# Parked-table writes moved from ScalarE's queue to SyncE's, and one row scaling moved from ScalarE to VectorE, in a vision-tower kernel

## What is computed

```python
lu, ru, ld, rd = _shifts(x)                          # four diagonal shifts by half a patch
concat = jnp.concatenate((x, lu, ru, ld, rd), axis=1)
normed = (concat - mean) * rsqrt(var + EPS)          # one mean and variance per image
normed = normed * gamma[None] + beta[None]
y = conv_general_dilated(normed, W, (8, 8), 'VALID') + b    # 169 patches, 128 features
h = concatenate([cls_tok, y])                        # 170 tokens
h = h + attention(layernorm(h))                      # S += LR * v k^T per token; out = S q
h = h + ffn(layernorm(h))
```

## Time and profile before

| | |
|---|---|
| Median of 3 runs | 220.32 us (219.75 to 221.87) |
| The profiled execution's own time | 220.32 us |
| Its span, first to last instruction | 218.1 us |
| Outside the span | 2.2 us |
| TensorE busy | 197.3 us (90%) |
| GpSimd / VectorE / ScalarE busy | 153.8 / 152.9 / 127.6 us |
| Mean granted clock of TensorE | 0.982 of full speed |

### The profile page before, as it was taken

One profiled execution on the slowest core, in us unless ns is written; L12 is line 12 of the kernel. 1 busy time (PEld: TensorE's weight loads), 2 busy tenths in 40 slices (PEclk: granted clock), 3 DMA queues, 4 the chain that ended last, 5 costly groups with the idle time before them and its releaser, 6 DMA issues.

```text
span 218.1 us, 5079 instructions
## 1 busy us (share of the span) xinstructions
PE 197.3 (90%) x1566; PEld 168.0 (77%) x1566; DVE 152.9 (70%) x762; ACT 127.6 (59%) x312; POOL 153.8 (70%) x129
## 2 busy tenths in 40 slices
PE   0699997998999999999999999999999999999820
PEld 0489895886888889888888888889988888888610
DVE  4548875480576685769686687796696686699892
ACT  4322545699433545556755575745755565677982
POOL 1029946697993799969899939957999632445571
PEclk9999999999999999999999999999999999999975
DMA  5999992931305004234135252022022022010356
GB/s 142 388 424 420 416 423 86 221 165 28 150 0 165 5 3 162 54 87 148 31 70 187 47 169 50 3 50 51 0 48 51 2 51 48 19 32 3 77 120 150
DMA packets 17074, 25.90 MB, mean 119 GB/s; under 512 B 1576, under 2 KB 13551, under 8 KB 16920
## 3 DMA queue, kind: packets, MB, share of 16 engines
q1 hardware_dynamic: 16300, 25.06, 36.0%
q10 hardware_dynamic: 748, 0.51, 0.8%
HBM read 19.65 MB, written 5.92 MB: 117 GB/s over the span
## 4 chain that ended last, share of the span: by engine, by line
PE 69%; DVE 9%; DMA 9%; SPq 3%; issue 3%; POOL 3%; ACT 1%; POOLq 0%; ACTq 0%; DVEq 0%
PE conv L560 34%; PE vr_ps L608 12%; DMA images<-x_rows 9%; PE first_ps L618 9%; PE outs L635 8%; PE turn L593 4%; DVE dve L1232 2%; DVE state L983 2%; DVE state L975 2%; PE conv L568 1%; ACT scaled L773 1%; DVE images L1004 1%; POOL rstd L1325 1%; SPq L477 1%; DVE ln_stats L1012 1%
## 5 line engine op out<-in xcount | busy, mean ns | idle before, releaser
L560 PE MATMUL conv<-scaled,wt 128*128 128x256 f32 (+3 forms) x432 | 111.5, 374 | 7.4 <-DMA wt<-weight 7.1
L460 POOL TENSOR_TENSOR scaled<-rows,gam 128x832 f32<-128x832 f32 (+1 forms) x54 | 83.9, 1574 | 18.1 <-DMA rows<-x_windows 17.9
L560 PEld LDWEIGHTS conv<-scaled,wt 128*128 128x128 f32 x432 | 71.7, 193 | 15.4 <-DMA wt<-weight 7.1
L803 ACT ACTIVATE values<-vr_ps,rstd 128x256 f32<-128x256 f32 x76 | 36.0, 474 | 60.5 <-PE vr_ps L608 50.3
L1309 POOL TENSOR_TENSOR rstd<-var,powers 128x8 f32<-128x8 f32 (+2 forms) x20 | 30.4, 1519 | 26.6 <-DVE var L995 26.4
L975 DVE TENSOR_TENSOR state<-first_ps,state 128x128 f32<-128x128 f32 x76 | 22.1, 291 | 29.9 <-PE first_ps L618 25.0
L811 ACT ACTIVATE images<-images,ln_shift,ln_gain 128x128 f32<-128x128 f32 x80 | 37.3, 489 | 1.5 <-DVE ln_shift L1052 0.7
L1299 POOL TENSOR_TENSOR g_low<-g_t,g_high 128x512 fp32r<-128x512 f32 x21 | 26.7, 1273 | 7.0 <-ACT g_high L790 7.0
L608 PE MATMUL vr_ps<-w_high,g_low 128*128 128x256 f32 x77 | 30.7, 398 | 1.0 <-ACT values L803 0.9
L964 DVE BATCH_NORM_STATS2 ln_stats<-images 128x6 f32<-128x128 f32 x85 | 23.6, 285 | 5.1 <-ACT images L797 5.0
L983 DVE TENSOR_TENSOR state<-second_ps,state 128x128 f32<-128x128 f32 x76 | 21.5, 283 | 2.1
(11 more groups left out here) (197 smaller groups left out, 276.5 us busy)
## 6 DMA issues: line engine op xcount, KB each, us to landing
rows<-x_windows SPq DMA_DIRECT2D x12, 864.0 KB, 5.1
out<-images SPq DMA_DIRECT2D x40, 128.0 KB, 2.4
images<-x_rows SPq DMA_DIRECT2D x4, 832.0 KB, 14.7
images<-x_rows SPq DMA_DIRECT2D x1, 1040.0 KB, 14.1
images<-x_rows SPq DMA_DIRECT2D x1, 624.0 KB, 21.1
rows<-x_windows SPq DMA_DIRECT2D x1, 448.0 KB, 6.2
gam<-gamma SPq DMA_DIRECT2D x1, 422.5 KB, 7.0
bet<-beta SPq DMA_DIRECT2D x1, 422.5 KB, 7.5
```

What stands on the lines that cost most here:

```text
L460: return eng.tensor_tensor(scaled[:, s, at + skip:at + N], window[:, skip:N], gains.unsqueeze(2).to_broadcast([P, N - skip, B]), ALU.mult)
L560: last = pe.matmul(conv_ps[g % 2][:, at:at + n * B], held, scaled[:, s, a % RING:a % RING + n], start=first, stop=(g < EARLY and s >= TOP ...
L803: act.activation(values[:, t % VALUE_SLOTS].rearrange("p a e -> p (a e)"), vr_bank(t)[:, 0:2 * E], ACT.Identity, scale=rho_of(t)).then_inc ...
```

## The change

Two edits that don't touch each other. ScalarE no longer issues the two parked writes; SyncE does, behind the loads of rows 3 and 4 and ahead of its wait for them. And (4, 4) is no longer scaled by ScalarE token by token in the steps -3, -2 and -1, but by VectorE with one instruction in step -2, with a semaphore of its own (scaled_by_vector). (4, 3) stays on ScalarE.

```diff
-BY_SCALAR = ((2, 4), (3, 4), (4, 3), (4, 4))
+BY_SCALAR = ((2, 4), (3, 4), (4, 3))
+BY_VECTOR = ((4, 4),)
-ROW_4_TOKENS = {-7: (3, 0, 5), -6: (3, 5, 4), -4: (3, 9, 4), -3: (4, 0, 4), -2: (4, 4, 4), -1: (4, 8, 5)}
+ROW_4_TOKENS = {-7: (0, 5), -6: (5, 4), -4: (9, 4)}
...
             if (last, s) in BY_SCALAR:
                 eng.wait_ge(scaled_by_scalar, BY_SCALAR.index((last, s)) + 1)
+            elif (last, s) in BY_VECTOR:
+                eng.wait_ge(scaled_by_vector, 1)
...
             load_row(3)
             load_row(4)
+            for blk in range(2):
+                count = P if blk == 0 else PATCHES - P
+                sp.wait_ge(table_low_ready, blk + 1)
+                sp.dma_start(parked[blk * P:blk * P + count], term_parts[0:count, blk].bitcast(F32)).then_inc(terms_parked, 16)
             sp.wait_ge(terms_zero, 1)
             sp.wait_ge(terms_parked, 32)
...
             act.copy(w_high[:], w_vr[:]).then_inc(w_high_ready, 1)
-            for blk in range(2):
-                count = P if blk == 0 else PATCHES - P
-                act.wait_ge(table_low_ready, blk + 1)
-                act.dma_start(parked[blk * P:blk * P + count], term_parts[0:count, blk].bitcast(F32)).then_inc(terms_parked, 16)
             group_out(1)
...
+                if t == -2:
+                    for r, s in BY_VECTOR:
+                        dve.wait_ge(row_in[r % ROW_SLOTS], 16 * (r // ROW_SLOTS + 1))
+                        dve.wait_ge(gamma_in, 16)
+                        dve.wait_ge(conv_step, SHIFTS * last_group_of_row(r - 2) + s + 1)
+                        scale_shift(dve, r, s).then_inc(scaled_by_vector, 1)
```

More of the change, by code:

```diff
@@ L153, in pool_scales @@
 def pool_scales(r, s):
-    return SHIFTS * (r - 1) + s + 1 - len([at for at in BY_SCALAR if at <= (r, s)])
+    return SHIFTS * (r - 1) + s + 1 - len([at for at in BY_SCALAR + BY_VECTOR if at <= (r, s)])
 FIRST_SCALES = (-7, -5, -4, -3, -2)
@@ L171 @@
 LATE_SCALES = [(r, s, scale_step(r, s)) for r in range(EARLY_ROWS, N) for s in range(SHIFTS)
-               if (r, s) not in BY_SCALAR + ((N - 1, BOTTOM + 1),)]
+               if (r, s) not in BY_SCALAR + BY_VECTOR + ((N - 1, BOTTOM + 1),)]
 def tower(nc, x_rows, x_windows, first_offsets, first_gamma, gamma, beta, weight, top_weight, last_row, smalls, bias, owners, cls_tok,
@@ L315, in tower @@
         scaled_by_scalar = sem("scaled_by_scalar")
+        scaled_by_vector = sem("scaled_by_vector")
         corner_scaled = sem("corner_scaled")
@@ L470, in load_row @@
                     sp.wait_ge(scaled_by_scalar, len([at for at in BY_SCALAR if at[0] <= r - 3]))
+                    if r - 3 >= EARLY_ROWS:
+                        sp.wait_ge(scaled_by_vector, 1)
                     if r - 3 >= CORNER // N:
@@ L840, in step @@
                 if t in ROW_4_TOKENS:
-                    s, first, count = ROW_4_TOKENS[t]
+                    first, count = ROW_4_TOKENS[t]
                     for j in range(first, first + count):
-                        last = scale_part(EARLY_ROWS, s, j)
+                        last = scale_part(EARLY_ROWS, SHIFTS - 2, j)
                     if first + count == N:
```

## The result

The changed kernel takes 218.88 us (median of 20 runs), the kernel before 220.19 us on the same chip; the ratio is 0.9933, 95% interval 0.9912 to 0.9954. So it gains 0.67% by the ratio and 1.31 us by the medians, where 2.06 were forecast (the ratio is not the quotient of the two medians). One of the 20 runs took 403.51 us and is not in the ratio; without it the median is 218.84. The profiled execution has a span of 216.8 us, 1.3 less than before.

The account below looks back on a forecast made before the run. TensorE was taken as the bound from 52 to 190 us, carrying any earlier start to the end. 1.1 + 0.96 = 2.06 us off 220.32 gave 218.3 us (chance 0.46), range 217.6 to 219.6.

Parts of the forecast that it names:

- Part 1: Ahead of the statistics: writes issued behind row 4 let chunk 4 land earlier, 1.1 us gained, bounds 0.64 to 1.24.
- the ceiling: At chunk 4: VectorE, busy with chunk 3 until 27.60, limits the gain from earlier landing to 1.24 us.
- Rival 2: Image loads don't land earlier, something other than the writes held chunk 4: 219.4 us, chance 0.14.
- the 1.1: Gain in us taken ahead of chunk 4, near the upper bound: the engine carrying both writes is the last one.
- its second term: Ahead of chunk 4: the 82 KB write, on one DMA engine, costs that engine 0.6 us more.
- Part 2: At vr of tile 4: (4, 4) on VectorE brings its start from 51.65 to 50.69, 0.96 us gained, lower bound 0.7.
- rival 1: Around tile 5: GpSimd held up to 1.03 us by VectorE's new instruction, 0.77 us lost, 219.0 us, chance 0.25.
- margin: At vr of tile 5: values of tile 4, behind GpSimd's root of group 1, come in time by 0.26 us.
- a sign of being wrong: On TensorE after 52 us: a new gap there would show the prediction wrong; no size given.
- Rivals 3 and 4: Terms late, TensorE stalls 2.85 us: 221.1, chance 0.04; other waits replace both, neither edit tells: 220.0, chance 0.06.
- the two terms of the sum: Gains of 1.1 us ahead of the statistics and 0.96 us at vr of tile 4, together 2.06 us.

Follow-up runs that it names:

- the experiment: Kernel before with only the 82 KB write moved behind the loads of rows 3 and 4, the 256 KB write left early: 220.01 us, ratio 1.0003.
- the two parts alone: Kernel before with only the two writes moved to SyncE behind row 4: 219.51 us; with only (4, 4) scaled on VectorE: 219.55 us.

## Why the prediction was right or wrong

**Part 1** was right in mechanism and size: 1.22 us by the trace for 1.1 (bounds 0.64 to 1.24). VectorE became the ceiling as worked out, chunks 5 and 6 stayed hidden, row 3 came earlier by as much, and the wait for the writes ended at 36.98 as expected. Rival 2, that something else held the chunk, falls with the late writes of ScalarE: the same writes 8 us later give the same gain. The sums stand at 33.84 with ScalarE issuing late and at 33.81 with SyncE, so it was their time that counted.

The working took a chunk to have landed when its slowest engine is done. The trace records a chunk's landing as 16 signals, without the engine of each: in the kernel before, those of chunk 4 come from 26.30 to 28.82 us, and VectorE starts on it at 28.84; in the changed kernel they end at 27.59.

The working beneath the 1.1 was wrong, though. It put 0.64 us on the large write's share and 0.6 on the small one sitting on one engine. The runs put all of it on the large write. Its share in the experiment was 26.4% of 2.5 us, 0.66 us of each engine, and still the sums were 1.2 us late. Of the missing half the runs show only that it falls on chunks 4 and 5 together; that some engines got more of it than others is one possible reason, and was not shown. So the 1.1 came near 1.22 partly by luck: its second term, 0.6 for the small write, stood in for a loss that the large write caused. The small write's one engine was real (6.9% of 16 engines for its last 2 us). With that write moved, chunk 4 was taken 0.5 us earlier, but chunk 5 held VectorE in its place, and neither the sums nor the time gained.

**Part 2** was sized right up to vr of tile 4: 0.98 us for 0.96 by the second matmul. The step that failed is the one behind it, GpSimd's hold, which the sum put at nothing and rival 1 named. GpSimd's scaling took 0.78 us longer, and by the second matmuls vr of tile 5 came 3.12 us behind vr of tile 4, where the version with the gammas in PSUM has 2.51, so 0.61 us of the gain was lost. That is rival 1, at its place; both its terms were off, a hold of 0.78 for 1.03 and a margin of 0.17 (0.78 - 0.61) for 0.26, and its loss of 0.77 was 0.16 too large. Rival 1 had a chance of 0.25 and gave 219.0, near the measured 218.9 where the forecast was 218.3. That its time fits so closely is partly luck: it left 0.19 us of part 2, the trace has about 0.4 left at 60 us, and the loss of 0.25 behind it, which no rival named, makes up most of the difference. What spoke for the forecast, that VectorE might be the one to wait, was half true. By the rows VectorE's instruction ended 0.9 us after GpSimd's g_low, and GpSimd's next one 1.44 us after VectorE's, which reads as VectorE waiting first and then holding GpSimd's next instruction in its turn. With two SBUF inputs the rows took 1.65 and 2.36 us, with one 1.01 and 1.58.

**Behind 52 us** the prediction took TensorE to carry any lead to the end, and named as a sign of being wrong a gap there that was not there before. There is one of 0.2 us, and the lead falls by 0.25 us at it, because GpSimd's run from 71 to 95 us has no slack and VectorE's stream had grown a delay ahead of it. 1.22 + 0.98 - 0.61 - 0.25 = 1.34 us; the trace shows 1.38 at the end and the medians 1.31.

Rivals 3 and 4 fall: no wait of TensorE for terms, and both parts tell. The forecast that the change would most likely stay within 1% held (0.67%), and the range of 217.6 to 219.6 held the time because it reached to rivals 1 and 2. The PSUM version, with neither the hold nor the late loss, shows what the two terms of the sum are worth: a lead of 2.10 us at 60 us for 2.06, of which 1.08 is part 1 (sums at 33.95) and 1.02 part 2.

What stays open beside the causes named: the two parts alone gain 0.43 and 0.39 us by their medians, together 0.8 (1.1 by the ratios), where the whole gains 1.3 (1.5 by the ratio); the intervals of the ratios are wide enough for both to be true, and no run tells more.

## What to carry to other kernels

Before an elementwise step goes to an idle VectorE, look at what GpSimd does in that stretch and how many of the step's inputs lie in SBUF: with two, an instruction of 1.03 us cost GpSimd 0.78 us here, and the root behind GpSimd's work paid. Moving it to where GpSimd idles, or putting the small input in PSUM, took the cost away (GpSimd back to 1.58 us from 2.36). Two writes that nobody needed for 20 us, issued behind the loads that VectorE waited for, brought the sums 1.22 us forward; which queue they stood in did not matter here (33.84 us and 33.81).

## What the runs showed of the hardware

A write that takes 0.66 us of each DMA engine's time delayed the image loads' last use by 1.2 us (sums at 35.02 for 33.81). The 82 KB write of 41 partitions ran on about one engine (6.9% of 16); with it alone early the sums came 0.4 us later, at 34.22, of which 0.27 stood ahead of chunk 3 already, and in time it could not be told from none (219.28 us for 219.51 and 219.6). Of two instructions that held each other, both rows in the profile get longer (1.65 for 1.03, 2.36 for 1.58), which reads as if a row's start were not the start of its work; the sum of the two excesses, 1.40 us, is not what either path lost. A VectorE stream had a delay of 0.1 to 0.4 us (at most 0.79 for a usual step of 0.41) at a place that moved with the number of instructions ahead of it, waits included.
